# Placing the preparation of an LSTM: rounding w_proj, turning block 0's attention output, and the order of the work around them

## The chip, the cores and the metric

One NeuronCore of one Trainium2 chip. The metric is the device time of one execution in microseconds, the median of several runs. A core has five engines with instruction queues of their own, each worked off strictly in the order in which the kernel wrote it: TensorE (PE, matrix products), VectorE (DVE), ScalarE (ACT, the activation functions), GpSimd (POOL) and SyncE (SP, which here only issues DMAs). They are tied together by semaphores: a producer adds to one when it ends, a consumer waits until it has reached a value.

## The reference, cut to what matters

The input `x` has 16 sequences of 128 positions with 128 features. Everything below is computed in one kernel.

```
x = x + attn(cond(x, cond_1024, W_cond), w_qkv, w_proj, q_gain)
x = x + ffn(lstm(x, h0 = cond_1024, Wx, Wh, b), ...)

cond:  (x * ys) @ W * rsqrt(ys^2 @ W^2 + 1e-8)              ys = cond / sqrt(128)
attn:  qkv = x @ ternary(w_qkv).T      16 query heads, 4 key/value heads, 8 wide
       q, k = rms_norm(q), rms_norm(k);  rotary embedding;  q *= q_gain
       y = causal softmax(q k / sqrt(8)) v
       out = rms_norm(y) @ ternary(w_proj).T
ternary(w): w in bfloat16, in groups of 64: s = mean|w|, round(w / s) held to -1..1, times s
lstm:  a = x_t @ Wx + b + h @ Wh
       c = sigmoid(f) * c + sigmoid(i) * tanh(g);  h = sigmoid(o) * tanh(c)     128 steps
ffn:   int8 fake quantisation, silu(x @ w_gate) * (x @ w_up), again, @ w_down
```

What counts for this case is the order that the data force: step t of the LSTM needs the attention's output at position t, and its own output of step t - 1. So the 128 steps are one chain, and it can begin as soon as the attention is done for the first positions.

## The kernel before, in words

The 128 positions are cut into four blocks of 32. A block holds 32 positions of all 16 sequences, 512 tokens, as four tiles of 128 tokens (four sequences each). Block 0's attention is done ahead of the recurrence; blocks 1 to 3 are done as side work between the steps of the recurrence, by hand-written tables that say at which step each piece is issued (`KEYS_AT`, `ROWS_AT`, `EXP_AT` and so on). No planner is involved: the order of each engine's queue is the order of the Python lines. The change touches only the part ahead of the loop over steps, and one thing of step 0.

**Block 0's way to the first step.** TensorE computes scores twice. The first (`score_rows`, L1195 to L1199) only serve the row maxima, which VectorE takes (`maxima`, L1760). The second (`score_cols`, L1241 to L1250) have the maxima taken off, ScalarE makes their exponentials (`exps`, L863), and `weigh_0` (L1263) multiplies them by the values: 16 products, group g outermost and tile T innermost, each of two passes, so that tile T's sum is complete in the last quarter, tiles 0 to 3 in turn. `pv_done` counts these. `turn_0(T)` on VectorE (L1769 to L1774) waits for `pv_done`, transposes the tile in 32 x 32 squares and inverts the softmax's sum. `normalise(0, T)` on GpSimd (L625) multiplies by the inverse. `y_square(0, T)` on ScalarE (L887) sums the squares, in two instructions. `row_norms(0)` on GpSimd (L595, L600) waits for all four and takes the inverse root. Then the tiles are scaled (`yn_tok`: L895 on ScalarE, L1883 on VectorE), transposed by TensorE (`turn_block`, L1325), copied (`ynT`, L900 and L1887), and multiplied by the projection weight (`project_0`, L1340, first the 8 positions needed soonest, then the other 24). `residual_0(0)` on VectorE (L1783) adds x and gives `x1T`, and `fill_piece` (L1356) multiplies it by `Wx`, onto the bias and h0's part that are already in the bank. That releases the first gates' tanh on ScalarE (L1089), and with it step 0.

**What shares the queues with it.** VectorE rounds `w_proj` (`ternary(PROJ_C, n)`, nine dependent instructions, L1644 to L1666; its load is asked for at 6.2 us), finds the power of two that scales the LSTM's weights (L1864 to L1872: `wexp`, `gate_f`, `factor_ready`) and does block 1's norms of heads (`head_norm(1, n)`, n = 0 to 12, each dependent on the one before), its rotary sum (`turn_add`), its scaling (`scale_heads`) and the low halves of its float16 pairs (`lower`). GpSimd does the bias (L677 to L681), the low half of Wh (`wh_lo`, L683), and the other half of block 1's rotary sum (L689). ScalarE scales Wh and Wx by `gate_f` (L954, L960, each a piece of 384 and one of 128 columns), and writes block 1's high halves (`upper(1, h, part)`, two instructions each, L824 to L828; they wait for `scale_heads(1, h)` by `rotated`) and block 2's values (`values_out(2, h)`, L768). `zeros_early(n)` on TensorE (L1362) are products of zeros whose results nobody reads.

## Time and profile before

| | us |
|---|---|
| median of 3 runs | 303.14 |
| lowest, highest | 301.21, 305.03 |
| the profiled execution | 304.36 |
| its span, from first to last instruction | 302.6 |
| mean granted TensorE clock over the span | 0.966 of 2.4 GHz |

Busy time: TensorE 264.2 us (87%, the products of zeros included), VectorE 211.1 (70%), ScalarE 185.5 (61%), GpSimd 69.1 (23%). The first gates' tanh, the start of the recurrence, begins at 46.12 us; what comes before it is the stretch that the change edits.

All times below are us from the start of the span. A row of a list in order of time gives the start, the busy time, the engine, the line of the kernel, the operation, what it writes and reads, and, where the engine had been idle, for how long and whose work ended that. Neighbouring instructions of one kind are merged ("x4"), and one instruction's time can overlap the next one's, since an engine starts an instruction before the one ahead has drained.

### The profile page before, as it was taken

Reading aid. Unit: us, or ns where it says so; the run is one execution under the profiler, and the core shown is the slowest. Engines: PE = TensorE matmul, PEld = TensorE weight load, DVE = VectorE, ACT = ScalarE, POOL = GpSimd, SP = SyncE. Lnnn points to the kernel's source line nnn. Section 1 sums busy time; section 2 is a strip of 40 time slices with the busy share of each in tenths; the row PEclk is TensorE's granted clock in tenths of the full one; section 3 lists DMA queues with packets and bytes.
Section 4 is the critical chain, followed back from the end, with each engine's and each line's share of the span. In section 5 each row is a group of like instructions: output and inputs, shape, how many; then the busy total and the mean of one; then the engine's idle time right before and its main releaser. Section 6 shows DMA issues by size and latency. Waiting matters only on the chain.

```text
span 302.6 us, 9175 instructions
## 1 busy us (share of the span) xinstructions
PE 264.2 (87%) x3436; PEld 156.7 (52%) x3436; DVE 211.1 (70%) x1041; ACT 185.5 (61%) x585; POOL 69.1 (23%) x107
## 2 busy tenths in 40 slices
PE   8658986999988898999998999999888888888894
PEld 2435744556665565665664655555434444433341
DVE  6787888786658777676678777555666565546985
ACT  7679857657778877567555666554224324545943
POOL 5712424591021058610110011002000000000630
PEclk9987999799899999599999999999999999999999
DMA  3434101000001000000000000000000000000004
GB/s 78 150 88 113 34 0 37 3 2 2 3 3 37 2 2 2 4 0 3 2 2 3 3 2 0 2 3 2 1 2 3 0 2 0 3 0 2 0 0 139
DMA packets 7498, 5.59 MB, mean 18 GB/s; under 512 B 1696, under 2 KB 6304, under 8 KB 7456
## 3 DMA queue, kind: packets, MB, share of 16 engines
q1 hardware_dynamic: 7168, 4.89, 6.1%
q8 instruction: 27, 0.44, 0.6%
q10 hardware_dynamic: 288, 0.13, 0.2%
q14 instruction: 15, 0.12, 0.1%
HBM read 2.40 MB, written 1.05 MB: 11 GB/s over the span
## 4 chain that ended last, share of the span: by engine, by line
PE 44%; DVE 30%; ACT 15%; issue 6%; POOL 3%; DMA 1%; DVEq 0%; SPq 0%; ACTq 0%; POOLq 0%
PE bank L1455 15%; PE bank L1474 8%; ACT tanh_c L1094 6%; DVE prod L1958 5%; DVE gates_sb L1961 5%; ACT gates_sb L1089 5%; DVE h_hi L1967 4%; DVE neg_max L1760 4%; PE bank L1297 2%; PE bank L1552 2%; PE bank L1356 2%; PE bank L1577 2%; PE bank L1241 1%; DVE h_lo L1972 1%; PE bank L1351 1%
## 5 line engine op out<-in xcount | busy, mean ns | idle before, releaser
L1474 PE MATMUL bank<-ident_b,zero_w 128*128 128x512 bf16 x274 | 81.9, 392 | 0.0
L1089 ACT ACTIVATE gates_sb<-bank 128x64 f32<-128x64 f32 x128 | 28.6, 224 | 53.2 <-PE bank L1455 52.8
L1455 PEld LDWEIGHTS bank<-h_hi,wh_hi 128*128 128x128 f16 x508 | 22.5, 97 | 63.3 <-DVE h_hi L1967 58.0
L1958 DVE SCALAR_TENSOR_TENSOR prod<-gates_sb 128x32 f32<-128x32 f32 x128 | 24.7, 193 | 41.7 <-ACT gates_sb L1089 38.8
L1094 ACT ACTIVATE tanh_c<-gates_sb 128x16 f32<-128x16 f32 x128 | 27.6, 216 | 39.2 <-DVE gates_sb L1961 36.9
L1455 PE MATMUL bank<-h_hi,wh_hi 128*128 128x16 f16 x508 | 32.8, 173 | 17.8 <-DVE h_hi L1967 16.7
L1967 DVE TENSOR_TENSOR h_hi<-o_scaled,tanh_c 128x16 f16<-128x16 f32 x127 | 22.3, 176 | 24.6 <-ACT tanh_c L1094 24.3
L1474 PEld LDWEIGHTS bank<-ident_b,zero_w 128*128 128x128 bf16 x274 | 23.7, 99 | 18.6 <-issue 8.8
L1455 PE MATMUL bank<-h_lo,wh_hi 128*128 128x16 f16 x508 | 32.6, 172 | 0.0
L863 ACT ACTIVATE probs<-bank,gain_max 128x512 f32<-128x512 f32 (+1 forms) x44 | 29.4, 676 | 3.1 <-PE bank L1250 2.7
L1455 PE MATMUL bank<-h_hi,wh_lo 128*128 128x16 f16 x508 | 31.0, 169 | 0.0
L1356 PE MATMUL bank<-x1T,wx_sb 128*128 128x128 f32 x128 | 29.9, 320 | 0.7 <-DVE x1T L1783 0.7
L1760 DVE TENSOR_REDUCE neg_max<-bank 128x4 f32<-128x384 f32 (+3 forms) x44 | 27.7, 635 | 1.6 <-PE bank L1199 1.6
L589 POOL TENSOR_TENSOR qk_r<-qk_r,minus_half 128x40 f32<-128x40 f32 x4 | 27.0, 6744 | 0.3
L1961 DVE SCALAR_TENSOR_TENSOR gates_sb<-prod 128x16 f32<-128x16 f32 x128 | 22.5, 176 | 4.4
L1972 DVE TENSOR_TENSOR h_lo<-hidden,h_hi 128x16 f16<-128x16 f32 x127 | 22.2, 175 | 4.4
L1455 PEld LDWEIGHTS bank<-h_lo,wh_hi 128*128 128x128 f16 x508 | 21.2, 96 | 2.9
L627 POOL TENSOR_TENSOR y_tok<-y_turn,recip 128x128 f32<-128x128 f32 x12 | 4.9, 411 | 75.7 <-DVE recip L1780 75.7
L726 POOL TENSOR_TENSOR h_ffn<-xT_sb 96x512 f32<-96x512 f32 (+1 forms) x4 | 5.0, 1268 | 74.2 <-ACT xT_sb L1116 74.2
L1963 DVE TENSOR_SCALAR o_scaled<-gates_sb 128x16 f32<-128x16 f32 x128 | 21.7, 170 | 0.0
L1455 PEld LDWEIGHTS bank<-h_hi,wh_lo 128*128 128x128 f16 x508 | 21.7, 96 | 0.0
L1969 DVE TENSOR_TENSOR hidden<-o_scaled,tanh_c 128x16 f32<-128x16 f32 x128 | 21.6, 168 | 0.2 <-ACT tanh_c L1094 0.2
(244 smaller groups left out, 479.2 us busy)
## 6 DMA issues: line engine op xcount, KB each, us to landing
xT_sb<-xT SPq DMA_DIRECT2D x4, 256.0 KB, 3.9
v_all<-v_tok SPq DMA_DIRECT2D x12, 64.0 KB, 2.1
outT<-probs SPq DMA_DIRECT2D x3, 256.0 KB, 2.5
wh_sb<-Wh SPq DMA_DIRECT2D x1, 256.0 KB, 3.6
v<-v_tok SPq DMA_DIRECT2D x8, 32.0 KB, 1.9
wx_sb<-Wx SPq DMA_DIRECT2D x1, 256.0 KB, 2.8
v<-yn_tok SPq DMA_DIRECT2D x8, 32.0 KB, 2.4
v_all<-yn_tok SPq DMA_DIRECT2D x4, 64.0 KB, 2.5
```

The costliest lines, as they stand in the source:

```text
L589: then_qk(G.tensor_tensor(qk_r[:, c, 0, hs], qk_r[:, c, 1, hs], minus_half[:, :].broadcast_to([P, NH * n]), ALU.pow))
L863: A.activation(probs[0:keys, n % 2, g, :], bank[COL_BANKS[k][g]][0:keys, :], ACT.Exp, scale=gain_max[0:keys, 2:3]).then_inc(probs_ready, 1)
L1089: A.activation(gates_sb[:, now, 0:GATES * B], bank[(t // BANK_STEPS) % 2][:, slot:slot + GATES * B], ACT.Tanh, scale=scale).then_inc(gates ...
L1094: A.activation(tanh_c[:, :], gates_sb[:, nxt, GATES * B:], ACT.Tanh, scale=0.5).then_inc(tanh_done, 1)
L1356: return E.matmul(out, wx_sb[:, g * P:(g + 1) * P], x1T[:, chunk * BANK_STEPS:(chunk + 1) * BANK_STEPS, :], start=False, stop=False, skip_ ...
L1455: ins = E.matmul(bank[dst][:, col:col + B], w[:, g * P:(g + 1) * P], h[:, part, :], start=False, stop=True, skip_group_check=True)
L1474: E.matmul(bank[1 - ((t + 1) // BANK_STEPS) % 2][:, :], zero_w[:, :], ident_b[:, :].unsqueeze(1).broadcast_to([P, 4, P]), start=False, sto ...
L1760: V.tensor_reduce(neg_max[:, per * u:per * (u + 1), g], bank[ROW_BANKS[k][g]][:, 0:per * keys].rearrange("p (b k) -> p b k", b=per), AX.X, ...
L1958: V.scalar_tensor_tensor(out=prod[:, :], in0=G[:, now, 0:2 * B], scalar=1.0, in1=G[:, now, 3 * B:5 * B], op0=ALU.add, op1=ALU.mult).then_i ...
L1961: V.scalar_tensor_tensor(out=G[:, nxt, 4 * B:5 * B], in0=prod[:, B:2 * B], scalar=0.5, in1=prod[:, 0:B], op0=ALU.mult, op1=ALU.add).then_i ...
L1967: V.tensor_tensor(h_hi[:, now, :], o_scaled[:, :], tanh_c[:, :], ALU.mult).then_inc(hidden_hi, 1)
L1972: V.tensor_tensor(h_lo[:, now, :], hs, h_hi[:, now, :], ALU.subtract).then_inc(hidden_lo, 1)
```

## The change

On VectorE the nine instructions that round `w_proj` move ahead: six of them (n = 0 to 5) stand before the row maxima, two (6, 7) between the sum of squares of block 1's first half and `lowered_out`, the last (8) before the maximum of Wh is read. The first three of block 1's norms of heads are put between the instructions that form `wexp`. `turn_0` now follows `gate_f` at once, and the rest of the norms follows it: n = 3 to 10 before the scaling of y, 11 and 12 right after it. At the end `scale_heads(1, 0)` stands ahead of `residual_0(0)`, and `lower(1, 0)` ahead of `modulated(3)`.

On GpSimd the rotary sum of block 1's first half moves from between the normalisations to a place ahead of the bias, and the low half of Wh moves from ahead of `normalise(0, 0)` to behind `normalise(0, 1)`.

On ScalarE the four `y_square(0, T)` are spread among the two scalings of Wx and the two copies out of bank 5; `upper(1, 0, 0)`, `upper(1, 0, 1)`, `upper(1, 1, 0)`, `upper(1, 1, 1)` are issued half by half; and `values_out(2, 0)` and `values_out(2, 1)` move from ahead of the recurrence to step 0, behind its first tanh.

On TensorE three of the four products of zeros ahead of `turn_block(0)` go.

```diff
--- before.py
+++ after.py
@@ -671,6 +671,11 @@
                 gp.wait_ge(ld_x[k], 16)
                 G.tensor_tensor(mod_x[:, k, :, :], xT_sb[:, k, :, :], ysT[:, :].unsqueeze(2).broadcast_to([P, B, ROWS]),
                                 ALU.mult).then_inc(modx_pool, 1)
+            gp.wait_ge(rotated, 2)
+            gp.wait_ge(trig_ready, 1)
+            first = slice(0, TILES * NH // 2)
+            G.tensor_tensor(heads_of(rot, 1)[:, first, :], heads_of(rot, 1)[:, first, :], sin_part[:, 1, first, :],
+                            ALU.add).then_inc(turned_qk, 1)
 
             gp.wait_ge(ld_bias, 16)
             gp.wait_ge(factor_ready, 1)
@@ -679,15 +684,10 @@
             then(G.tensor_tensor(bias_g[:, 1, :], bias_g[:, 0, :], bias_part[:, 0, :], ALU.subtract))
             then(G.tensor_copy(bias_part[:, 1, :], bias_g[:, 1, :]))
             G.tensor_tensor(bias_part[:, 2, :], bias_g[:, 1, :], bias_part[:, 1, :], ALU.subtract).then_inc(bias_ready, 1)
+            normalise(0, 0)
+            normalise(0, 1)
             gp.wait_ge(wh_cast, 1)
             G.tensor_tensor(wh_lo[:, :], wh_sb[:, :], wh_hi[:, :], ALU.subtract).then_inc(wh_split, 1)
-            normalise(0, 0)
-            normalise(0, 1)
-            gp.wait_ge(rotated, 2)
-            gp.wait_ge(trig_ready, 1)
-            first = slice(0, TILES * NH // 2)
-            G.tensor_tensor(heads_of(rot, 1)[:, first, :], heads_of(rot, 1)[:, first, :], sin_part[:, 1, first, :],
-                            ALU.add).then_inc(turned_qk, 1)
             normalise(0, 2)
             normalise(0, 3)
             row_norms(0)
@@ -955,30 +955,33 @@
             ac.wait_ge(wh_scaled, 2)
             A.activation(wh_hi[:, :], wh_sb[:, :], ACT.Copy).then_inc(wh_cast, 1)
             A.activation(h0_f[:, :], cond_sb[:, :], ACT.Copy, scale=H_SCALE).then_inc(h0_ready, 1)
+            y_square(0, 0)
             ac.wait_ge(ld_wx, 16)
-            for part, i in GATE_SCALES:
-                A.activation(wx_sb[:, part], wx_sb[:, part], ACT.Copy, scale=gate_f[:, 2 + i:3 + i]).then_inc(wx_scaled, 1)
-            y_square(0, 0)
+            part, i = GATE_SCALES[0]
+            A.activation(wx_sb[:, part], wx_sb[:, part], ACT.Copy, scale=gate_f[:, 2 + i:3 + i]).then_inc(wx_scaled, 1)
+            y_square(0, 1)
             ac.wait_ge(biasT_psum, 1)
             A.activation(twT[:, 2, :], bank[5][:, 3 * P:3 * P + P // 2].bitcast(BF16), ACT.Copy).then_inc(proj_T_ready, 1)
             A.activation(bias_T[:, :], bank[5][0:PARTS * GATES, PAIRS * NV:PAIRS * NV + P // 2].bitcast(BF16),
                          ACT.Copy).then_inc(biasT_ready, 1)
-            for T in range(1, TILES):
-                y_square(0, T)
+            y_square(0, 2)
+            part, i = GATE_SCALES[1]
+            A.activation(wx_sb[:, part], wx_sb[:, part], ACT.Copy, scale=gate_f[:, 2 + i:3 + i]).then_inc(wx_scaled, 1)
+            y_square(0, 3)
             qkv_out(2, 0)
             qkv_out(2, 1)
             y_scale(0, 0)
             y_scale(0, 2)
             ynT_out(0)
             square(2)
-            upper(1, 0, 0)
-            upper(1, 1, 0)
             for h in range(2):
+                upper(1, h, 0)
                 upper(1, h, 1)
-            values_out(2, 0)
-            values_out(2, 1)
 
             def side_a(t):
+                if t == 0:
+                    values_out(2, 0)
+                    values_out(2, 1)
                 for k in (2, 3):
                     for n, (at, place) in enumerate(trig_of(k)):
                         if (t, 0) == (at, place):
@@ -1432,7 +1435,7 @@
                 E.matmul(bank[0][:, g * B:(g + 1) * B], wh_sb[:, g * P:(g + 1) * P], h0_f[:, :],
                          start=False, stop=False, skip_group_check=True)
             claim(1)
-            zeros_early(4, 1)
+            zeros_early(1, 1)
             turn_block(0)
             zeros_early(1, 1)
             project_0(0)
@@ -1848,6 +1851,9 @@
             v.wait_ge(ld_wh, 16)
             V.tensor_reduce(wmax[:, 0:1], wh_sb[:, :], AX.X, ALU.max, apply_absolute_value=True).then_inc(wmax_ready, 1)
             queries_out(0, 3)
+            v.wait_ge(ld_proj, 16)
+            for n in range(6):
+                ternary(PROJ_C, n)
             for g in range(KV):
                 maxima(0, 0, g)
             v.wait_ge(maxed, KV)
@@ -1856,43 +1862,47 @@
             v.wait_ge(max_hi, 1)
             V.tensor_tensor(m_stack[:, :, :, 3 * HD + 1], neg_max[:, :, :], m_stack[:, :, :, 3 * HD], ALU.subtract).then_inc(max_lo, 1)
             sum_squares(1, 0)
+            ternary(PROJ_C, 6)
+            ternary(PROJ_C, 7)
             lowered_out(0, 1)
             lowered_out(0, 3)
             sum_squares(1, 1)
             modulated(2)
+            ternary(PROJ_C, 8)
             v.wait_ge(wmax_all, 1)
             V.tensor_reduce(wmax[:, 1:2], bank[4][:, 0:P], AX.X, ALU.max).then_inc(wmax_read, 1)
             v.wait_ge(wmax_read, 1)
-            then(V.tensor_scalar(wexp[:, 0:1], wmax[:, 1:2].bitcast(I32), 23, None, ALU.logical_shift_right))
-            then(V.tensor_scalar(wexp[:, 0:1], wexp[:, 0:1], -1.0, 266.0, ALU.mult, ALU.add))
-            then(V.tensor_scalar(wexp[:, 0:1], wexp[:, 0:1], 187.0, 20.0, ALU.min, ALU.max))
+            mark(V.tensor_scalar(wexp[:, 0:1], wmax[:, 1:2].bitcast(I32), 23, None, ALU.logical_shift_right))
+            head_norm(1, 0)
+            v.wait_ge(dve, done[0])
+            mark(V.tensor_scalar(wexp[:, 0:1], wexp[:, 0:1], -1.0, 266.0, ALU.mult, ALU.add))
+            head_norm(1, 1)
+            v.wait_ge(dve, done[0])
+            mark(V.tensor_scalar(wexp[:, 0:1], wexp[:, 0:1], 187.0, 20.0, ALU.min, ALU.max))
+            head_norm(1, 2)
+            v.wait_ge(dve, done[0])
             then(V.tensor_scalar(wexp[:, 1:2], wexp[:, 0:1], -1.0, 254.0 - 13.0, ALU.mult, ALU.add))
             mark(V.tensor_scalar(wexp[:, 2:3], wexp[:, 1:2], 23, None, ALU.logical_shift_left))
             then(V.tensor_scalar(wexp[:, 3:4], wexp[:, 0:1], 23, None, ALU.logical_shift_left))
             V.tensor_scalar(gate_f[:, :], gate_k[:, :], factor, None, ALU.mult).then_inc(factor_ready, 1)
-            v.wait_ge(ld_proj, 16)
-            for n in range(9):
-                ternary(PROJ_C, n)
             for T in range(TILES):
                 turn_0(T)
-            for n in range(8):
+            for n in range(3, 11):
                 head_norm(1, n)
             v.wait_ge(y_link, Y_OPS)
             v.wait_ge(v_moved[1], VALUES_MOVED[1])
             for T in (1, 3):
                 V.tensor_scalar(yn_tok[:, T, :], y_tok[:, T, :], rms_y[:, 2, T:T + 1], None, ALU.mult).then_inc(yn_ready_v, 1)
-            head_norm(1, 8)
-            head_norm(1, 9)
+            for n in range(11, QK_OPS):
+                head_norm(1, n)
             v.wait_ge(ynT_psum, 2)
             V.tensor_copy(ynT[:, BTOK // 2:], bank[YN_BANKS[0][1]][:, 0:BTOK // 2]).then_inc(ynT_ready_v, 1)
-            for n in range(10, QK_OPS):
-                head_norm(1, n)
             turn_add(1, 1)
+            scale_heads(1, 0)
             residual_0(0)
-            scale_heads(1, 0)
             scale_heads(1, 1)
+            lower(1, 0)
             modulated(3)
-            lower(1, 0)
             lower(1, 1)
 
             def side(t):
```

## Rows read from the trace of the kernel before

**Rows 1.** The page's part 4: the chain of waits, shares of the span by line
```profile
PE bank L1455 15%; PE bank L1474 8%; ACT tanh_c L1094 6%; DVE prod L1958 5%; DVE gates_sb L1961 5%; ACT gates_sb L1089 5%; DVE h_hi L1967 4%; DVE neg_max L1760 4%; PE bank L1297 2%; PE bank L1552 2%; PE bank L1356 2%; PE bank L1577 2%; PE bank L1241 1%; DVE h_lo L1972 1%; PE bank L1351 1%
```

**Rows 2.** Stretches of TensorE: us, busy (instructions), granted clock share, DMA
```profile
54.50:57.50 3.00, 3.00 (x22) 0.51 0.03 5
```

**Rows 3.** In order of time, ScalarE, recurrence: start us, us, engine, line, operation
```profile
53.64 0.22 ACT L1089 ACTIVATE gates_sb<-bank 128x64 f32<-128x64 f32 x1 [0.76 <-PE bank L1455]
...
57.98 0.22 ACT L1089 ACTIVATE gates_sb<-bank 128x64 f32<-128x64 f32 x1 [0.55 <-PE bank L1455]
...
59.74 0.22 ACT L1089 ACTIVATE gates_sb<-bank 128x64 f32<-128x64 f32 x1 [0.19 <-PE bank L1455]
```

**Rows 4.** In order of time, VectorE, 24 to 29 us (in brackets: idle before, releaser)
```profile
24.32 2.49 DVE L1760 TENSOR_REDUCE neg_max<-bank 128x16 f32<-128x512 f32 x4 [1.63 <-PE bank L1199]
...
28.33 1.29 DVE L1766 CAST h_ffn<-bank 128x512 f16<-128x512 f32 x2 [0.49 <-PE bank L1217]
```

**Rows 5.** In order of time, VectorE, 32 to 35.5 us
```profile
32.34 0.23 DVE L1872 TENSOR_SCALAR gate_f<-gate_k,wexp 128x8 f32<-128x8 f32 x1
...
33.78 0.23 DVE L1656 TENSOR_SCALAR tw<-tw_r 128x128 int8<-128x128 bf16 x1
...
34.77 0.72 DVE L1772 STREAM_TRANSPOSE y_turn<-bank 128x512 f32<-128x512 f32 x1
```

**Rows 6.** In order of time, TensorE, block 0's products
```profile
31.57 3.84 PE L1263 MATMUL bank<-probs,v 128*128 128x128 f32 x32
```

**Rows 7.** In order of time, GpSimd, 34 to 40 us
```profile
34.76 1.16 POOL L683 TENSOR_TENSOR wh_lo<-wh_sb,wh_hi 128x512 f16<-128x512 f32 x1 [0.68 <-ACT wh_hi L956]
...
37.08 0.86 POOL L689 TENSOR_TENSOR rot<-rot,sin_part 128x320 f32<-128x320 f32 x1
37.90 0.95 POOL L625 TENSOR_TENSOR y_tok<-y_turn,recip 128x128 f32<-128x128 f32 x2
39.37 0.19 POOL L595 TENSOR_SCALAR rms_y<-y_sum 128x4 f32<-128x4 f32 x1 [0.52 <-ACT y_sq L887]
```

**Rows 8.** In order of time, ScalarE, 33 to 46.4 us
```profile
33.11 0.91 ACT L954 ACTIVATE wh_sb<-wh_sb,gate_f 128x384 f32<-128x384 f32 x2
...
39.10 0.19 ACT L887 ACTIVATION_READ_ACCUMULATOR y_sq<-y_tok 128x1 f32 x1
...
44.09 0.26 ACT L824 ACTIVATE k_stack<-rot 128x64 f16<-128x64 f32 x1 [1.43 <-DVE rot L1737]
...
45.91 0.31 ACT L768 ACTIVATE v_tok<-bank 128x64 f32<-128x64 f32 x2
46.12 0.21 ACT L1089 ACTIVATE gates_sb<-bank 128x64 f32<-128x64 f32 x1
```

**Rows 9.** Groups by line, shapes apart, ScalarE: busy us, mean ns, idle before
```profile
L960 ACT ACTIVATE wx_sb<-wx_sb,gate_f 128x128 f32<-128x128 f32 x1 | 0.4, 386 | 0.0
```

**Rows 10.** One line of the kernel: duration ns min/median/max, first and last start us
```profile
L1700 DVE TENSOR_SCALAR qk_r<-qk_r x2: 202/330/457, 14.2 to 38.4; 128x80 int32<-128x80 int32 x2
```

**Rows 11.** In order of time, VectorE, 41.9 to 44.5 us
```profile
41.94 0.42 DVE L1887 COPY ynT<-bank 128x256 f32<-128x256 f32 x1 [0.31 <-PE bank L1325]
...
42.97 0.48 DVE L1727 TENSOR_TENSOR rot<-rot,sin_part 128x320 f32<-128x320 f32 x1
43.37 0.37 DVE L1783 TENSOR_TENSOR x1T<-bank,xT_sb 128x128 f32<-128x128 f32 x1
43.58 0.87 DVE L1737 TENSOR_TENSOR rot<-rot,qk_r 128x320 f32<-128x320 f32 x2
```

**Rows 12.** In order of time, TensorE, 39 to 45.1 us
```profile
39.13 1.02 PE L1362 MATMUL bank<-zero_w 128*128 128x512 bf16 x4
41.17 0.73 PE L1325 MATMUL bank<-ident_f,yn_tok 128*128 128x128 f32 x4 [1.01 <-ACT yn_tok L895]
...
43.46 0.38 PE L1362 MATMUL bank<-zero_w 128*128 128x512 bf16 x1
43.88 1.13 PE L1356 MATMUL bank<-x1T,wx_sb 128*128 128x128 f32 x8
```

## The prediction

> **What bounds the kernel now.** I began with the page's chain of waits. It spends most of the span in the lines of the recurrence [rows 1], a chain that the change leaves alone, so what the change is worth is how much sooner step 0's first tanh runs; everything behind it is placed by step number and moves along. That tanh begins at 46.12 us [rows 8], and I then read each engine in order of time from 22 us to there.
>
> Two things release it. One is data: y of block 0 is turned, normalised, projected and multiplied by Wx, and the last of these products runs from 43.88 to 45.01 [rows 12]. The other is ScalarE's own queue: it sits idle 1.43 us until VectorE has scaled block 1's heads, begins block 1's high halves at 44.09, then does block 2's values at 45.91, and only then the tanh, 1.1 us after its data were there [rows 8]. So ScalarE's queue is the wait that ends last, and the chain of data is 1.1 us behind it.
>
> **Rounding w_proj.** From the end of `gate_f` (32.57) to the start of the first turn (34.77) VectorE does nothing but the nine instructions of the rounding, 2.2 us; the first six end at 34.01, so they take about 1.5 us [rows 5]. The new place has a wait of 1.63 us for the scores, which covers the six with 0.1 us over. Two more, 0.5 us by the time between 34.01 and the turn, meet a wait of 0.49 us [rows 4]; the last, 0.2 us, I put under a further short wait for TensorE. Cost 0 to 0.2 us; I take 0. If the cover at 24 us shrank (products faster there), up to 1 us would be late, and the row maxima, on which everything waits, with them.
>
> **What the 2.2 us buy.** `turn_0(0)` can't begin before tile 0's last product. The 32 passes of `weigh_0` run from 31.57 to 35.41, 0.12 us each, and tile 0 is complete three tiles, six passes, before the end: 35.41 - 0.72 = 34.69 [rows 6]. The first turn began at 34.77 [rows 5]. So the rounding hid almost entirely in a wait that the list doesn't show, because VectorE was not idle; with it gone VectorE waits instead. Gain at the turns: 0 to 0.1 us, I take 0. The four turns and inverses then run as before, one after the other.
>
> **wexp with the norms between.** Three norms are added ahead of `gate_f`, of which the first and the third fit between dependent instructions and the second is the long one. It took 202 ns once and 457 ns the other time [rows 10]; the second time it began while GpSimd normalised y (0.95 us from 37.90) [rows 7]. `gate_f` comes 0.3 us later, at 32.9. ScalarE begins to scale Wh at 33.11, behind its exponentials [rows 8]: hidden with 0.2 us over. GpSimd's bias comes 0.3 us later and ends near 34.4, ahead of y. The rotary sum of 0.86 us [rows 7] falls in GpSimd's idle time ahead of the bias: 0.
>
> **GpSimd.** In place of the rotary sum (37.08, 0.86 us) the low half of Wh (1.16 us) stands before `normalise(0, 2)` [rows 7]. That is 0.3 us more; the third normalisation runs from 38.2 to 38.6 rather than from 37.90, the fourth ends at 38.97 instead of 38.85. Tile 0 and 1 gain 0.04 us at most and nobody profits. Cost so far: 0.12 us.
>
> **ScalarE's squares.** The small piece of Wx's scaling (386 ns, about 0.30 us from start to start [rows 9]) now stands between the third square and the fourth. The third begins at 38.65, holds the engine 0.3 us, the piece 0.3 us, so the fourth begins at 39.25 though its data are there at 39.0. GpSimd's inverse root, 0.52 us behind the fourth normalisation before (38.85 to 39.37) [rows 7], comes at 39.25 + 0.49 = 39.74. The chain of y is 0.37 us late. The large piece and the copies out of bank 5 lie in waits for y and cost the bias on TensorE 0.1 us, ahead of slack.
>
> **From the inverse root to x1.** The scaling, the transposes and the copy shift by 0.37 us: the `ynT` copy ends at 42.73 instead of 42.36 [rows 11]. Before, three norms (0.8 us) and the rotary sum stood between it and the residual. Now `turn_add` (0.40 us to the next) and `scale_heads(1, 0)` (0.4 us) stand there: the residual ends at 43.77 against 43.74 [rows 11]. The 0.37 us are given back to 0.03. TensorE, 0.37 us later, starts its product of zeros at 43.83 instead of 43.46 and can start Wx's products 0.21 us behind it, at 44.05 instead of 43.88 [rows 12]. They take 1.13 us: first gates ready at 45.2.
>
> **ScalarE's queue at the end.** `scale_heads(1, 0)` now ends at 43.48, where the pair ended at 44.45 (its first half at 44.0) [rows 11]. `upper(1, 0, 0)` can begin at 43.52 instead of 44.09. All four of them take 45.91 - 44.09 = 1.82 us [rows 8], so they are done at 45.35; the second half of the heads is scaled by 44.1, before its turn comes. Values (46.12 - 45.91 = 0.21 us) move behind the tanh, into ScalarE's wait for the cell. The tanh begins at 45.37 instead of 46.12. VectorE, with its two `lower` and `modulated(3)`, is done at 45.65, as the tanh hands over. DMAs of block 2's values go out later by under 1 us and are needed tens of steps on. **Sum: -0.75 us**, of which 0.21 are the values and 0.57 the earlier halves, less rounding.
>
> Bounds: if the chain of y is not late at all, the four halves start 0.37 us sooner and the gain is 1.1 us; if GpSimd and VectorE hold each other, it is 0.4 us. The second comes from the row with the two durations: 457 - 202 = 255 ns for one meeting [rows 10]. In the new order norms with two inputs run beside `normalise(0, 2)` and `(0, 3)`. I take no further delay, since most norms ran undisturbed beside the inverse root.
>
> The Trainium skill, SBUF — State Buffer, Who interferes with whom, says that GpSimd and VectorE share a pair of ports that one instruction holds whole, and that a VectorE instruction with two SBUF inputs contends with a GpSimd one that reads SBUF. The long duration agrees with blocking; by that rule the sum would be nearer -0.5 us than -0.75.
>
> **From the sum to the time.** The profiled execution took 304.36 us for a span of 302.6. It would be 303.6. It is 1.2 us above the median of the runs; from the median, 303.14 - 0.75 = 302.4 us.
>
> **Rivals.** *Nothing gained.* The late y chain and meetings on the ports add up to 0.4 us more, or a wait behind step 0 (values, keys, sums of squares) takes the head start: 303.1 us. For it: the change adds work to the y chain at two places. Against: 1.1 us lay between data and tanh. Chance 0.22.
>
> *The turns do start earlier.* If the modelled ends of products are late, or `weigh_0` itself starts sooner, the turns gain up to the 2.2 us between `gate_f` and the first of them, less the 0.3 us of norms: 302.4 - 1.9 = 300.5 us. Against: the product's count above lands 0.08 us before the turn. Chance 0.08.
>
> *Slower: the clock falls.* TensorE loses three products of zeros (about 0.64 us of 1.02), so its gap before the transposes grows from 1.01 to about 2.0 us [rows 12]. In the trace the granted clock is at 0.51, the 1.2 GHz level, from 54.5 to 57.5 us [rows 2], after the gaps around step 0. If it fell at 42 us instead, transposes (0.73), zeros and Wx's products (1.13) and the projection ahead of them, some 2.5 us of TensorE on the path, would take twice as long: +2.5 - 0.75 = +1.75, 304.9 us. It decides only if the fall comes between 41.5 and 45.2. Against: a gap of 1.01 us there brought none. Chance 0.12.
>
> The Trainium skill, TensorE: Matmul & The Clock Gate, What's actually happening, states that the array's clock goes back to the lower level when it has been idle. By that rule removing the zeros speaks against this change; the trace's fall after step 0's gaps agrees, and that its place differs from one execution to the next no row here can show.
>
> **How the numbers follow.** Forecast 0.58, nothing 0.22, slower 0.12, turns earlier 0.08. Falls of the clock in the recurrence set the scatter: two steps across one took 57.98 - 53.64 = 4.34 us, an undisturbed one 59.74 - 57.98 = 1.76, so a fall costs 0.8 us [rows 3], and their number may change with any shift. The three runs lie 1.9 us to either side of the median. The range takes that on both sides of 302.4: from 300.4, which also takes in nearly all of the case of earlier turns, to 304.6, which holds the case of nothing gained and part of the slower one. Faster or slower by over 2%, about what a measurement can tell from no change, would be under 297.1 or over 309.2. No case reaches either; a mistake in the mechanism or a fortunate or bad set of falls leaves 0.04 and 0.02. Within 2%: 0.94.
>
> **What would show it.** VectorE idle from about 32.9 to 34.75 and the first turn still near 34.8; `wh_lo` between the second and third normalisation; the inverse root's first instruction near 39.7 rather than 39.37; the first residual's end near 43.8; the first tanh near 45.4, directly behind the last high half. Wrong: a first turn well before 34.6, row maxima starting later than 24.3, a granted clock of 0.5 between 41 and 46, or a first tanh after 46.

## The result, and where the time went

| | before | changed |
|---|---|---|
| median of 20 runs, us | 304.34 | 308.00 |
| lowest, highest | 300.85, 306.01 | 304.10, 311.98 |
| profiled execution, its span | 304.36, 302.6 | 308.47, 306.7 |

The ratio is 1.0115, 95% interval 1.0082 to 1.0148: the changed kernel is slower by 1.15%, less than 2% but clear of the scatter of twenty runs each. The forecast was 302.4 us, in a range of 300.4 to 304.6. (Runs over 1.5% above the fastest of their kernel are left out of the ratios, 6 of the changed kernel's 20, 5 of e4's 14 and 5 of e2's 12 below, so a ratio can differ from the quotient of the medians.)

In these two profiled executions the whole difference arises before the recurrence. From the first gates' tanh to the last it takes 229.26 us before and 229.19 after (that the two agree so well is luck: in the profiles of the experiments below the same stretch took 227.5 to 234.0 us); the first tanh begins at 50.30 us instead of 46.12. The 4.18 us come in three pieces: 2.84 until the first turn of y (37.61 against 34.77 [rows 5]), 0.44 from there to the inverse root (5.04 against 4.60 us), 0.90 from there to the tanh (7.65 against 6.75).

**The first piece.** VectorE and GpSimd of the changed kernel, in order of time:

```profile
24.06 2.48 DVE L1763 TENSOR_REDUCE neg_max<-bank 128x16 f32<-128x512 f32 x4
...
27.50 1.14 DVE L1661 TENSOR_TENSOR tw_r<-tw,tw_s 128x128 bf16<-128x128 int8 x1
28.68 0.95 DVE L1663 TENSOR_TENSOR tw_r<-tw_r,tw_b 128x128 bf16<-128x128 bf16 x1
29.55 1.27 DVE L1769 CAST h_ffn<-bank 128x512 f16<-128x512 f32 x2
...
37.61 0.72 DVE L1775 STREAM_TRANSPOSE y_turn<-bank 128x512 f32<-128x512 f32 x1 [3.75 <-PE bank L1266]
```

```profile
27.45 2.10 POOL L672 TENSOR_TENSOR mods<-xT_sb,ysT 128x512 f32<-128x512 f32 x2 [11.20 <-DVE m_stack L1863]
```


The six instructions of the rounding ahead of the row maxima cost nothing: the maxima begin 0.81 us after the first scores (TensorE from 23.25 us), against 1.06 us before (from 23.26). Instructions 6 and 7 are another matter. They were expected to fill a wait of 0.49 us [rows 4] with 0.5 us; they take 1.14 and 0.95 us, beside two GpSimd instructions that multiply x by ys (2.10 us from 27.45, 1.05 and 1.10 us long). Instruction 6 ends 0.1 us behind the first of them, instruction 7 at 29.63, 0.1 us behind the second. The copies of the lowered queries start at 29.55 instead of 28.33 [rows 4], 1.22 us late. The same two GpSimd instructions stood there in the kernel before:

```profile
27.70 2.06 POOL L672 TENSOR_TENSOR mods<-xT_sb,ysT 128x512 f32<-128x512 f32 x2 [11.45 <-DVE m_stack L1857]
```

TensorE waits for the copies:

```profile
31.19 0.42 PE L1244 MATMUL bank<-h_ffn 32*32 32x128 f16 x32 [1.52 <-DVE h_ffn L1769]
...
32.78 5.47 PE L1266 MATMUL bank<-probs,v 128*128 128x128 f32 x32
...
44.49 1.12 PE L1328 MATMUL bank<-ident_f,yn_tok 128*128 128x128 f32 x4 [2.10 <-ACT yn_tok L895]
...
46.17 2.04 PE L1343 MATMUL bank<-ynT,twT 128*128 128x128 f32 x4
...
48.44 1.82 PE L1359 MATMUL bank<-x1T,wx_sb 128*128 128x128 f32 x8
```

```profile
33.90:36.60 2.70, 2.70 (x15) 0.54 0.02 5
42.00:43.00 1.00, 0.40 (x3) 1.00 0.00 0
43.00:44.00 1.00, 0.00 (x0) 0.61 0.00 0
44.00:49.90 5.90, 5.27 (x17) 0.50 0.00 0
```


The first fence is TensorE in order of time, the second its stretches (length, busy, granted clock, DMA). TensorE had been idle 1.52 us before the second scores, where before there was no gap. In block 0's products its clock is at 0.54, that is near 1.2 GHz, and they take 5.47 us instead of 3.84 [rows 6]. So 1.22 us of waiting became 1.22 + 1.63 = 2.85 us.

The gap is longer than 1.22 us because the changed kernel's trace had a small lead here that the change did not make. The two rows below are TensorE in the kernel before and in the changed one:

```profile
20.00:26.50 6.50, 5.46 (x104) 0.50 0.62 149
24.00:28.00 4.00, 2.57 (x60) 1.00 0.46 115
```


The kernel before computed its first scores at half clock, the changed one at full clock (as did e7, whose code is the old one there), and its maxima began 0.26 us sooner (24.06 against 24.32). Counted from the start of the maxima, the copies are 5.49 - 4.01 = 1.48 us late.

**The second piece** is what the prediction said: the small piece of Wx's scaling stands between the third and the fourth square. GpSimd and ScalarE in order of time:

```profile
39.92 1.16 POOL L690 TENSOR_TENSOR wh_lo<-wh_sb,wh_hi 128x512 f16<-128x512 f32 x1
41.03 0.88 POOL L625 TENSOR_TENSOR y_tok<-y_turn,recip 128x128 f32<-128x128 f32 x2
42.65 0.23 POOL L595 TENSOR_SCALAR rms_y<-y_sum 128x4 f32<-128x4 f32 x1 [0.74 <-ACT y_sq L887]
```

```profile
41.89 0.39 ACT L969 ACTIVATE wx_sb<-wx_sb,gate_f 128x128 f32<-128x128 f32 x1
...
48.42 0.40 ACT L828 ACTIVATE q_stack<-rot 128x256 f16<-128x256 f32 x1
50.30 0.22 ACT L1092 ACTIVATE gates_sb<-bank 128x64 f32<-128x64 f32 x1 [1.48 <-PE bank L1359]
```


**The third piece.** The last row has the sign of it: the tanh waits 1.48 us for Wx's products, so the data, not ScalarE's queue, end last. TensorE was idle 2.10 us before the transposes (1.01 before [rows 12]); the clock falls inside the gap, between 43 and 44 us, and stays at half until 49.9. The transposes take 1.12 us instead of 0.73, the projection 2.04 instead of 1.16, Wx's products 1.82 instead of 1.13 [rows 12]. The projection in the kernel before:

```profile
42.47 1.16 PE L1340 MATMUL bank<-ynT,twT 128*128 128x128 f32 x4 [0.35 <-issue]
```

### The profile page after: what moved, and what is told of

It reads as the page before. It is cut to its first block, busy times and chain, and to the rows that moved or that the text cites. A ratio compares the mean times of both kernels' runs of the same rounds, so it can differ in the third digit from the quotient of the medians.

```text
span 306.7 us, 9169 instructions
## 1 busy us (share of the span) xinstructions
PE 265.1 (86%) x3433; PEld 158.6 (52%) x3433; DVE 211.7 (69%) x1041; ACT 185.7 (61%) x585; POOL 68.9 (22%) x107
## 3 DMA queue, kind: packets, MB, share of 16 engines
HBM read 2.40 MB, written 1.05 MB: 11 GB/s over the span
## 4 chain that ended last, share of the span: by engine, by line
PE 46%; DVE 29%; ACT 14%; issue 5%; POOL 3%; DMA 1%; DVEq 0%; SPq 0%; ACTq 0%; POOLq 0%
PE bank L1458 15%; PE bank L1477 7%; ACT tanh_c L1097 6%; DVE prod L1968 5%; ACT gates_sb L1092 5%; DVE gates_sb L1971 5%; DVE h_hi L1977 4%; DVE neg_max L1763 4%; PE bank L1300 3%; PE bank L1359 2%; PE bank L1555 2%; PE bank L1580 2%; PE bank L1266 2%; PE bank L1244 1%; DVE h_lo L1982 1%
## 5 line engine op out<-in xcount | busy, mean ns | idle before, releaser
L1477 PE MATMUL bank<-ident_b,zero_w 128*128 128x512 bf16 x274 | 80.9, 388 | 0.0
L1359 PE MATMUL bank<-x1T,wx_sb 128*128 128x128 f32 x128 | 30.9, 330 | 0.7 <-DVE x1T L1786 0.7
```

Source lines behind the costliest of these rows:

```text
L1359: return E.matmul(out, wx_sb[:, g * P:(g + 1) * P], x1T[:, chunk * BANK_STEPS:(chunk + 1) * BANK_STEPS, :], start=False, stop=False, skip_ ...
L1477: E.matmul(bank[1 - ((t + 1) // BANK_STEPS) % 2][:, :], zero_w[:, :], ident_b[:, :].unsqueeze(1).broadcast_to([P, 4, P]), start=False, sto ...
```

## The experiments

Each kernel ran in five rounds of several executions beside the kernel before on the same chip, unless said; each has one profile. "Turn to tanh" is the time in its profile from the start of the first turn of y to the first gates' tanh: 11.35 us before, 12.69 changed.

| run | first turn | turn to tanh | first tanh | ratio to before (95%) |
|---|---|---|---|---|
| before | 34.77 | 11.35 | 46.12 | |
| changed | 37.61 | 12.69 | 50.30 | 1.0115 (1.0082 to 1.0148) |
| e1_round_late | 35.14 | 11.56 | 46.70 | 1.0006 (0.9966 to 1.0046) |
| e2_zeros_back | 39.00 | 12.09 | 51.09 | 1.0048 (1.0005 to 1.0090) |
| e3_both | 35.20 | 11.68 | 46.88 | 1.0010 (0.9971 to 1.0049) |
| e4_round_alone | 38.41 | 11.33 | 49.74 | 1.0038 (0.9990 to 1.0086) |
| e5_three_forms | 36.06 | 11.74 | 47.80 | one run, no ratio |
| e6_zeros_in_gap | 36.13 | 11.67 | 47.80 | 1.0095 (1.0056 to 1.0135) |
| e7_zeros_less_alone | 34.88 | 11.59 | 46.47 | 0.9984 (0.9949 to 1.0019) |
| e8_old_chain | 35.07 | 10.24 | 45.31 | 0.9960 (0.9924 to 0.9997) |
| e9_end_alone | 35.12 | 10.93 | 46.05 | 0.9972 (0.9936 to 1.0009) |
| e10_one_product | 36.69 | 12.78 | 49.47 | 1.0044 (1.0004 to 1.0085) |

The start of a profile shifts by up to 1.5 us from one execution to the next (the scores already stand later), so intervals within a profile are compared, not clock times.

### e1: the rounding's last three instructions elsewhere

```diff
             sum_squares(1, 0)
-            ternary(PROJ_C, 6)
-            ternary(PROJ_C, 7)
             lowered_out(0, 1)
...
             modulated(2)
-            ternary(PROJ_C, 8)
...
             V.tensor_scalar(gate_f[:, :], gate_k[:, :], factor, None, ALU.mult).then_inc(factor_ready, 1)
+            for n in range(6, 9):
+                ternary(PROJ_C, n)
             for T in range(TILES):
```

> The changed kernel, with the last three instructions of the rounding of w_proj (6, 7, 8) moved into VectorE's idle time between gate_f and the first turn. Theory A (VectorE's instructions 6 and 7, which read two tensors of SBUF, are held while GpSimd multiplies x by ys; the lowered queries, the scores and so TensorE are late, TensorE's idle time lets its clock fall during block 0's products): 6 and 7 take 0.3 and 0.2 us again in place of 1.14 and 0.95, the lowered queries' copy starts near 28.2 us instead of 29.55, the products take 3.84 us instead of 5.47 and the first turn starts at 34.5 to 34.8 instead of 37.61. Whether the clock still falls before the transposes (gap of 2 us) A leaves open: first tanh near 45.4 without (time 1 us under the kernel before), near 47.5 with (1 us over it). Theory B (the y chain's new order and the removed zeros cost the time): first turn at most 1 us earlier than 37.61, products still 5.4 us, time within 1 us of the changed kernel's, 3 to 4 us over the kernel before.

VectorE and TensorE in order of time:

```profile
28.69 1.29 DVE L1769 CAST h_ffn<-bank 128x512 f16<-128x512 f32 x2 [0.58 <-PE bank L1220]
...
32.92 0.28 DVE L1661 TENSOR_TENSOR tw_r<-tw,tw_s 128x128 bf16<-128x128 int8 x1
33.24 0.22 DVE L1663 TENSOR_TENSOR tw_r<-tw_r,tw_b 128x128 bf16<-128x128 bf16 x1
...
35.14 0.72 DVE L1775 STREAM_TRANSPOSE y_turn<-bank 128x512 f32<-128x512 f32 x1 [1.42 <-PE bank L1266]
```

```profile
31.93 3.84 PE L1266 MATMUL bank<-probs,v 128*128 128x128 f32 x32
...
42.02 1.12 PE L1328 MATMUL bank<-ident_f,yn_tok 128*128 128x128 f32 x4 [2.09 <-ACT yn_tok L895]
...
43.70 1.86 PE L1343 MATMUL bank<-ynT,twT 128*128 128x128 f32 x4
```


Theory A holds. The two instructions are back at 0.28 and 0.22 us, the products at 3.84, and VectorE even idles 1.42 us before the turn. The ratio goes from 1.0115 to 1.0006: the place of these three instructions is nearly the whole loss. The clock still falls before the transposes (1.12 us, after 2.09 us without work), and hands back what the new end had won: turn to tanh is 11.56 us against 11.35 before. But the fall is shorter than in the changed kernel: Wx's products run at full clock again (1.05 us, against 1.82), and from the inverse root to the tanh it takes 6.52 us against 7.65. So 1.13 of the changed kernel's 4.18 us went with the three instructions too, by a longer fall; whether they cause its length isn't shown (see e10).

### e4: the rounding's new place alone

```diff
             queries_out(0, 3)
+            v.wait_ge(ld_proj, 16)
+            for n in range(6):
+                ternary(PROJ_C, n)
...
             sum_squares(1, 0)
+            ternary(PROJ_C, 6)
+            ternary(PROJ_C, 7)
             lowered_out(0, 1)
...
             modulated(2)
+            ternary(PROJ_C, 8)
...
-            v.wait_ge(ld_proj, 16)
-            for n in range(9):
-                ternary(PROJ_C, n)
```

> The kernel before, with nothing changed but the place of the rounding: its nine instructions go where the changed kernel has them (six ahead of the row maxima, two ahead of the lowered queries, one ahead of Wh's maximum). Theory A: instructions 6 and 7 take about 1.1 and 0.95 us, the lowered queries start 1.2 us late, the products take 5.4 us because the clock falls in them, the first turn starts near 37.5 against 34.77, and the time is 2.5 to 3 us over the kernel before. Theory B: the rounding is hidden, the first turn stays near 34.8, time within 0.5 us of the kernel before.

Its VectorE and its TensorE in order of time:

```profile
28.30 1.14 DVE L1658 TENSOR_TENSOR tw_r<-tw,tw_s 128x128 bf16<-128x128 int8 x1
29.48 0.95 DVE L1660 TENSOR_TENSOR tw_r<-tw_r,tw_b 128x128 bf16<-128x128 bf16 x1
```

```profile
31.99 0.41 PE L1241 MATMUL bank<-h_ffn 32*32 32x128 f16 x32 [1.52 <-DVE h_ffn L1766]
...
33.58 5.47 PE L1263 MATMUL bank<-probs,v 128*128 128x128 f32 x32
```


The trace shows all of the first piece without any other part of the change: 1.14 and 0.95 us, the gap of 1.52, the products at 5.47. Before the transposes the gap is 1.00 us, and they take 0.73 us: with the four products of zeros and the old chain of y the second fall doesn't come. Over the runs the ratio is only 1.0038, some 1.2 us and not the 2.5 to 3 that I expected, and its interval reaches 1, so the price in time is less well shown here than the mechanism. The median of its runs is 306.80 us, against 304.67 of the kernel before beside it. The rounding's new place alone (1.0038) and the change without the collision (e1, 1.0006) add up to less than the changed kernel's 1.0115. The intervals are wide enough for a plain sum; whether the parts make each other worse isn't shown.

### e6: TensorE kept busy in the gap

```diff
             modulate(2)
+            claim(3)
+            zeros_early(6, 3)
             score_cols(0, 0, 0)
```

> The changed kernel, with six products of zeros on TensorE between block 2's modulation and the second scores, where it had been idle 1.5 us. Theory A (idle time lets the clock fall): the lowered queries are still 1.2 us late, but the clock stays at 2.4 GHz in block 0's products, which take 3.84 us instead of 5.47; first turn near 36.0, time about 1.6 us under the changed kernel. Theory C (the products are slow because something else competes with them, not by the clock, or the clock falls for a reason other than this gap): products still near 5.4 us, time unchanged.

Its TensorE in order of time:

```profile
29.66 1.46 PE L1365 MATMUL bank<-zero_w 128*128 128x512 bf16 x6
...
32.93 3.84 PE L1266 MATMUL bank<-probs,v 128*128 128x128 f32 x32
```


The copies are as late as in the changed kernel (instructions 6 and 7 still take 1.14 and 0.95 us), but the products take 3.84 us. So the clock, and the gap that let it fall, made the second half of the first piece. The time did not follow as expected: 1.0095, hardly under the changed kernel. Its recurrence took 234.0 us in the profile against 229.2, with more stretches at half clock in it (0.950 over the span). Why there are more of them is open.

### e5: which instructions are held

```diff
             sum_squares(1, 0)
-            ternary(PROJ_C, 6)
-            ternary(PROJ_C, 7)
+            mark(V.tensor_reduce(probe_s[:, 0:2], wn, AX.X, ALU.add))
+            mark(V.tensor_scalar(probe_8[:, :], tw_r[:, 2, :], 1.0, -1.0, ALU.min, ALU.max))
+            mark(V.tensor_tensor(probe_b[:, :], tw_r[:, 2, :], tw_b[:, 2, :], ALU.subtract))
             lowered_out(0, 1)
```

`wn` is `tw_b`'s part of w_proj in its groups; the rounding's three are behind `gate_f`.

> The changed kernel with the rounding's last three instructions behind gate_f, and three instructions into scratch tensors in the place beside GpSimd's multiplication of x: a sum over bfloat16 (one SBUF input, 0.29 us elsewhere), a clamp bfloat16 to int8 (one SBUF input, 0.23 us elsewhere), a difference of two bfloat16 tensors (two SBUF inputs, 0.22 us elsewhere). Their results are not used. Theory A (only what needs the second read port is held): the sum takes 0.3 us, the difference 0.7 to 1.1 us. The clamp tells whether a one-input instruction in a faster mode is held as well: 0.23 us if not, up to 1 us if so. Rival D (any VectorE instruction is slow there, or only the one with an int8 input was): all three slow, or none.

Its VectorE and its GpSimd in order of time:

```profile
27.64 0.28 DVE L1869 TENSOR_REDUCE probe_s<-tw_b 128x2 f32<-128x128 bf16 x1
27.83 0.88 DVE L1870 TENSOR_SCALAR probe<-tw_r 128x128 int8<-128x128 bf16 x1
28.63 1.08 DVE L1871 TENSOR_TENSOR probe_b<-tw_r,tw_b 128x128 bf16<-128x128 bf16 x1
```

```profile
27.58 2.05 POOL L675 TENSOR_TENSOR mods<-xT_sb,ysT 128x512 f32<-128x512 f32 x2 [11.44 <-DVE m_stack L1866]
```


The sum takes 0.28 us, undisturbed. The difference (two SBUF inputs) is held: 1.08 us. So is the clamp, which has one input but runs from bfloat16 to int8: 0.88 us, where it took 0.23 alone. So an int8 input isn't needed for a hold, and not every VectorE instruction suffers. The Trainium skill, SBUF — State Buffer, Who interferes with whom, says that a VectorE instruction with two SBUF inputs contends with a GpSimd instruction that reads SBUF, that one in a two-port mode contends too, that whoever issues first holds the shared ports for its whole instruction, and that a reduction never contends. The sum's 0.28 us and the difference's 1.08 agree with it. The clamp's 0.88 us agrees if it ran in such a mode, which no run here shows.

### e10: one GpSimd instruction taken from beside it

```diff
-            for k in (2, 3):
-                gp.wait_ge(ld_x[k], 16)
...
+            scaled_x(2)
             gp.wait_ge(rotated, 2)
...
                             ALU.add).then_inc(turned_qk, 1)
+            scaled_x(3)
```

`scaled_x(k)` is the body of the loop (L672).

> The changed kernel, with the rounding left where the change put it, but GpSimd's second multiplication of x by ys (block 3's, 1.03 us, not needed before 36 us) moved behind the rotary sum, so that only block 2's stands beside instructions 6 and 7 of the rounding. Theory A (VectorE is held exactly while a GpSimd instruction that reads SBUF runs): instruction 6 still takes about 1.1 us, instruction 7 falls from 0.95 to 0.22 us, the lowered queries start 0.7 us sooner than in the changed kernel, TensorE's gap falls from 1.52 to about 0.8 us, and if that is short enough for the clock, the products take 3.84 us and the first turn starts 2.3 us sooner (near 35.3); time about 2 us under the changed kernel's. Rival E (6 and 7 are slow by their own place, whatever GpSimd does): both keep 1.14 and 0.95 us, nothing moves.

Its VectorE, GpSimd and TensorE in order of time:

```profile
28.94 1.14 DVE L1663 TENSOR_TENSOR tw_r<-tw,tw_s 128x128 bf16<-128x128 int8 x1
30.11 0.22 DVE L1665 TENSOR_TENSOR tw_r<-tw_r,tw_b 128x128 bf16<-128x128 bf16 x1
...
32.44 0.57 DVE L1671 TENSOR_TENSOR tw<-tw_r,tw_b 128x128 bf16<-128x128 bf16 x1
```

```profile
28.89 1.05 POOL L672 TENSOR_TENSOR mods<-xT_sb,ysT 128x512 f32<-128x512 f32 x1 [11.51 <-DVE m_stack L1865]
32.08 0.86 POOL L678 TENSOR_TENSOR rot<-rot,sin_part 128x320 f32<-128x320 f32 x1 [2.15 <-ACT rot L812]
```

```profile
31.90 0.42 PE L1246 MATMUL bank<-h_ffn 32*32 32x128 f16 x32 [0.77 <-DVE h_ffn L1771]
...
33.49 3.84 PE L1268 MATMUL bank<-probs,v 128*128 128x128 f32 x32
```


The dose is halved and so is the effect: 6 keeps its 1.14 us, 7 falls to 0.22, TensorE's gap to 0.77 us, and the clock holds (3.84 us). Rival E is out: the same instruction in the same place of its queue is slow or not as GpSimd is busy or not. Instruction 8, untouched by the edit but now beside GpSimd's rotary sum, went from 0.21 to 0.57 us. From the start of instruction 6 to the first turn it takes 36.69 - 28.94 = 7.75 us, 2.36 less than the changed kernel's 10.11. The ratio is 1.0044. Turn to tanh stays at 12.78 us, with the long fall in it (Wx's products 1.91 us), although the clock held in block 0's products: the fall before the tanh came without one in the products, as in e1, e5 and e6.

### e7, e3 and e2: the products of zeros before the transposes

```diff
             claim(1)
-            zeros_early(4, 1)
+            zeros_early(1, 1)
             turn_block(0)
```

That is e7, on the kernel before. In e3 and e2 the reverse is done, on e1 and on the changed kernel.

> The kernel before, with three of the four products of zeros ahead of block 0's transposes taken away, as the changed kernel has it, and nothing else. Theory A: TensorE's gap grows from 1.0 to about 1.65 us; if that is enough, the granted clock falls to half from the transposes on and the first tanh comes up to 1 us later than 46.12 (but ScalarE's queue, 1.1 us behind the data there, hides most of it), so the time moves by 0 to 0.5 us. Theory B: no fall, first tanh at 46.1, time unchanged. The two differ in the trace (transposes 0.73 or 1.1 us), hardly in the time.

> The changed kernel with the rounding's last three instructions behind gate_f (as in e1) and the four products of zeros restored ahead of block 0's transposes. Theory A (two costs: VectorE held beside GpSimd, and the clock falling in the longer gap before the transposes): the gap there shrinks from 2.1 us to about 1.4, the transposes take 0.73 us again instead of 1.12, the projection 1.16 instead of 1.86, and from the first turn's start to the first tanh it takes about 10.7 us instead of e1's 11.56; time 0.8 us under e1's. Theory B (the gap is still long enough, or the fall has another cause): transposes still 1.1 us, 11.5 us from turn to tanh, time as e1's.

> The changed kernel with the four products of zeros restored ahead of the transposes, the rounding left in its new place. It completes the table with e1 and e3. By what e3 and e7 showed (clock falls after a gap of 1.45 or 1.65 us there, none after 0.79 or 1.00), the gap will be 1.45 us, the clock still falls and the time stays at the changed kernel's, 3 us over the kernel before. Theory Z (the removed zeros are the main cost): from the first turn to the first tanh about 11.4 us instead of 12.69, and the time 1 us or more under the changed kernel's.

TensorE in order of time, the transposes and the projection, in e7, e3 and e2:

```profile
41.27 0.73 PE L1325 MATMUL bank<-ident_f,yn_tok 128*128 128x128 f32 x4 [1.65 <-ACT yn_tok L895]
...
42.56 1.74 PE L1340 MATMUL bank<-ynT,twT 128*128 128x128 f32 x4 [0.35 <-issue]
```

```profile
42.09 1.10 PE L1328 MATMUL bank<-ident_f,yn_tok 128*128 128x128 f32 x4 [1.45 <-ACT yn_tok L895]
...
43.76 1.99 PE L1343 MATMUL bank<-ynT,twT 128*128 128x128 f32 x4
```

```profile
45.89 0.73 PE L1328 MATMUL bank<-ident_f,yn_tok 128*128 128x128 f32 x4 [1.45 <-ACT yn_tok L895]
...
47.19 1.87 PE L1343 MATMUL bank<-ynT,twT 128*128 128x128 f32 x4 [0.35 <-issue]
```


In e7 the gap is 1.65 us and the clock falls, from the projection on (1.74 us against 1.16). The tanh comes 0.24 us later after the turn; the rest is hidden in the 1.1 us for which ScalarE's queue held it anyway, and the time is that of the kernel before: 0.9984. In e3 the zeros came back and the clock fell all the same, with a gap of 1.45 us: my expectation was wrong, turn to tanh is 11.68 and not 10.7. The y chain is 0.45 us longer there than in the kernel before, so three products of zeros don't bring the gap back to 1.01 us. e2 has the same gap, and the clock falls a little later: the transposes still take 0.73 us, the projection 1.87. Turn to tanh, 12.09 us, lies between the two theories (12.69 and 11.4). Its ratio, 1.0048, is lower than I expected; its interval and the changed kernel's overlap only at their edges (1.0090 against 1.0082), but the two weren't run beside each other. The trace gives the zeros 0.6 us there; more isn't shown.

### e9: the new end alone

```diff
-            residual_0(0)
             scale_heads(1, 0)
+            residual_0(0)
             scale_heads(1, 1)
+            lower(1, 0)
             modulated(3)
-            lower(1, 0)
             lower(1, 1)
```

with the high halves by halves and the values in step 0, as in the change.

> The kernel before with the new end alone: scale_heads(1, 0) ahead of residual_0(0), the high halves half by half, lower(1, 0) ahead of modulated(3), block 2's values in step 0; the place of block 1's norms is the old one. By the prediction's step: ScalarE's queue was the wait that ended last, so the first tanh comes 0.5 to 0.7 us sooner after the first turn than the 11.35 us of before (less than the 0.75 us predicted, since three norms still stand ahead of the heads), time 0.5 us under the kernel before. Rival: the head start is given back at step 0 or 1 (block 2's values or the keys' transposes in the way): time unchanged, step 0 to step 2 longer than 3.5 us.

Turn to tanh takes 10.93 us, 0.42 less than before (expected 0.5 to 0.7), with a gap of 1.00 us before the transposes and the clock up, and the next tanhs follow at 1.80 and 1.77 us (1.75 and 1.76 before), so 0.06 us of it is handed back, not all. The ratio is 0.9972; its interval just reaches 1.

### e8: what is good of the change, with the old chain of y

```diff
+            gp.wait_ge(wh_cast, 1)
+            G.tensor_tensor(wh_lo[:, :], wh_sb[:, :], wh_hi[:, :], ALU.subtract).then_inc(wh_split, 1)
             normalise(0, 0)
             normalise(0, 1)
-            gp.wait_ge(wh_cast, 1)
-            G.tensor_tensor(wh_lo[:, :], wh_sb[:, :], wh_hi[:, :], ALU.subtract).then_inc(wh_split, 1)
...
-            zeros_early(1, 1)
+            zeros_early(5, 1)
             turn_block(0)
```

with both pieces of Wx's scaling ahead of `y_square(0, 0)` and the squares in one go, as before, and the rounding's instructions 6 to 8 behind `gate_f`, as in e1. The other parts of the change stay.

> The changed kernel, with the last three instructions of the rounding behind gate_f, five products of zeros ahead of the transposes, and the chain of y as before: both pieces of Wx's scaling ahead of the first square, and the low half of Wh ahead of the normalisations (the rotary sum of block 1 stays at its new early place). What is left of the change is six instructions of the rounding ahead of the row maxima, the norms between wexp's instructions, and the new end (heads by halves, values in step 0). Theory A: from the first turn to the first tanh 10.2 to 10.4 us (before: 11.35; e1: 11.56), no fall of the clock there, time 1.0 us under the kernel before. Theory B (the chain's order is without weight): as e3, 10.7 us.

Its TensorE and its ScalarE in order of time:

```profile
41.46 0.73 PE L1325 MATMUL bank<-ident_f,yn_tok 128*128 128x128 f32 x4 [0.79 <-ACT yn_tok L895]
...
42.76 1.19 PE L1340 MATMUL bank<-ynT,twT 128*128 128x128 f32 x4 [0.35 <-issue]
```

```profile
45.31 0.20 ACT L1089 ACTIVATE gates_sb<-bank 128x64 f32<-128x64 f32 x1
```


Turn to tanh takes 10.24 us, 1.11 less than before: 4.59 to the inverse root, as before, and 5.65 from there, against 6.75. The tanh follows directly behind the last high half, as the prediction had it. The gap is 0.79 us, the clock holds, the projection takes 1.19 us. Of the gap, the old chain is worth 0.45 us against e3 and the fifth product of zeros 0.2; with the old chain and four products (e4, e9) it was 1.00 us, and the clock held too. The median is 303.14 us against 304.22 beside it, ratio 0.9960 (0.9924 to 0.9997), the only version here whose interval lies under 1. That is an upper end of 0.9997 in one of nine intervals, so a gain of 0.4% over the kernel before is likely rather than shown. Against the changed kernel it is faster, by 1.5% if the two ratios are divided (they weren't run beside each other).

## Why the prediction was wrong

**What held.** Six instructions of the rounding fit in the wait for the scores. The turn doesn't profit from the rounding's leaving: e1 and e8 show VectorE idle 1.42 us ahead of it, waiting for the products. The y chain was forecast 0.37 us longer and is 0.44 longer (5.04 against 4.60), as in e1, e3, e6 and e10. The end was right in its mechanism: the inverse root at 39.74 and the tanh at 45.37 make 5.63 us, and e8, with the clock up, measures 5.65. Its bound for a y chain that isn't late at all, a gain of 1.1 us, is what e8 shows (1.11 from turn to tanh). The norms between wexp's instructions cost 0.08 us (1.41 against 1.33 us from the reading of Wh's maximum to `gate_f`) and not 0.3.

**The step that failed** is, in its section on rounding w_proj, "Two more, 0.5 us ..., meet a wait of 0.49 us ... Cost 0 to 0.2 us; I take 0." I looked for cover on VectorE's own row and not at what the other engines did in that same time. The two made the copies 1.22 us late (1.48 from the start of the maxima). The row that said so was in the prediction: an instruction of 202 ns that took 457 beside GpSimd [rows 10]; I set it against the norms beside `normalise`, where the traces show 0.1 us (0.32 and 0.33 us for two of them in the changed kernel and in e1, against 0.24), and not against the rounding, although the same GpSimd instructions stood in that stretch of the trace of before, from 27.70 to 29.76 us. Its growth of 255 ns, taken twice, would still have been too small against 0.86 + 0.73 us: every hold of the rounding's instructions and of e5's ended within 0.15 us of the end of GpSimd's instruction, so what bounds it is what is left of that one.

**The second error is the weight of the clock rival.** It had 304.9 us, 2.5 us over the forecast, and a chance of 0.12, for one fall before the transposes. That fall came, at the place given, and cost 2.0 us: 7.65 us from inverse root to tanh instead of 5.65 (transposes, projection and Wx's products grew by 0.39 + 0.88 + 0.69 = 1.96 us; in the trace of before they took 0.73, 1.16 and 1.13 us, which is 3.0 and not the prediction's 2.5, but they didn't quite double). So its price was fair and its chance too low. Even that price is in part luck: e10 shows the same (7.74 us), but e1, e3, e5 and e6, with the same new order of y's chain, got the clock back before Wx's products and paid 0.9 to 1.05 us (6.52 to 6.70). The argument against the rival, that a gap of 1.01 us brought no fall, was too weak: gaps of 0.77 to 1.01 us kept the clock in the traces here, gaps of 1.45, 1.65 and 2.10 us before the transposes did not. Length alone doesn't settle it, for a gap of 1.71 us ahead of step 1 in the kernel before was passed at full clock (1.00 from 47 to 53 us):

```profile
47.37 0.24 PE L1455 MATMUL bank<-h_hi,wh_hi 128*128 128x16 f16 x4 [1.71 <-DVE h_hi L1967]
```


And another fall, after the 1.52 us gap that the held instructions made, was not foreseen: 1.63 us in block 0's products. With both, 303.6 (the forecast for the profiled execution) + 1.22 + 1.63 + 2.0 = 308.5, against 308.47 measured. It closes so well only because the two recurrences happen to be equally long in these two profiles.

One smaller slip: the rival "nothing gained" puts 303.1 us on two ways, but its 0.4 us of late chain and meetings alone would leave 302.8.

**What stays open.** How often the clock falls in the recurrence changes from kernel to kernel and from run to run. From the start of the row maxima to the first tanh it took 21.80 us before, 26.24 in the changed kernel, 23.59 in e6 and 24.88 in e4, but the recurrence in the profiles of e6 and e4 took 234.0 and 233.4 us, and their ratios show less of the gain and of the loss than the first 50 us do. That the scatter goes with the clock is shown below; what decides where it falls, and how long, is not.

## What to carry to other kernels

Idle time of an engine is cover only for instructions that don't need what another engine holds at that time: before filling a VectorE wait, look at GpSimd's row in the same microseconds, and put there reductions (0.28 us beside it, as alone) or copies out of PSUM (1.29 us for the lowered queries beside GpSimd in the kernel before, 1.27 behind it in the changed one), not sums of two SBUF tensors, nor a clamp to int8. A stall of 1.5 us ahead of TensorE cost its length and then the half clock in what followed, which here more than doubled it; one of 0.8 us cost its length only (e5, e10). And an engine whose queue hid a delay stops hiding it once that queue is shortened: that three products of zeros can go from the old order without a measurable cost (e7) says nothing of the new one.

## What the runs showed of the hardware

A VectorE difference of bfloat16 tensors in SBUF, 0.22 us alone, took 0.95 to 1.08 us beside a GpSimd product of 1.05 to 1.10 us, and ended about 0.1 us behind it; a clamp from bfloat16 to int8 was held alike, a sum along the rows (a reduction, 0.28 us) was not. GpSimd's power of 128 x 4 values (1.04 us, from 39.65 in the kernel before and from 42.97 in the changed one) didn't hold the two-input norms beside it (0.24 us each).

The scatter of the runs goes with the granted clock (correlation 0.86 over the changed kernel's 20 runs). Of the changed kernel's 20 runs the fastest, 304.10 us, had a mean clock of 0.974 and the slowest, 311.98, had 0.944. Counting twice the missing share of the span as time at half clock, that is 15.7 and 34.7 us; a straight line through the 20 runs gives 0.34 us of time for each us at half clock, and 0.27 to 0.37 through the runs of the experiments. The median run had 24.5 us of it in the changed kernel, 16.9 in e8, and 14.5 to 18.2 in the kernel before beside the experiments. So the changed kernel's runs spend some 6 to 10 us more at half clock; by that line, an estimate, 2 to 3.4 us of its loss.
